# A decoder layer on one core: the w1/w3 products as seven block products for eight, w2 in a stage of its own, and the last normalisation moved into attention

## What is computed

```python
x = x + attn(layernorm(x), Wqkv, q_ln, k_ln, Wout)     # 32 heads of 32, ALiBi, causal
x = x + xattn(layernorm(x), ctx, Wq, Wk, Wv, Wo, bo, g) # softmax on q and k, normalised output
x = x + ffn(layernorm(x), w1, s1, w2, s2, w3, s3)

def ffn(x, ...):                 # dim 1024, hidden 2752, 4-bit weights, a scale for each 64
    a = einsum('bsd,hd->bsh', x, W1)
    b = einsum('bsd,hd->bsh', x, W3)
    return einsum('bsh,dh->bsd', silu(a) * b, W2)
```

## Time and profile before

| what | value |
|---|---|
| median of 3 runs | 3301.26 us (3300.97 to 3302.31) |
| span of the profiled execution | 3302.6 us |
| granted TensorE clock, mean | 0.976 of full |
| attention, one turn in the middle | 72.7 us |
| feed-forward stage | 1812.3 to 3302.6 us |
| PE / DVE / ACT / POOL busy | 95% / 54% / 32% / 15% |

### The profile page before, as it was taken

The page is one execution under the profiler, slowest core; times in us unless marked ns, Lnnn a source line. Parts: engine busy times, 40 slices in busy tenths (PEclk is TensorE's granted clock), DMA queues, the critical chain, the costliest instruction groups (busy, mean ns, idle before and its releaser), DMA issues. The chain is left out here.

```text
span 3302.6 us, 41842 instructions
## 1 busy us (share of the span) xinstructions
PE 3132.5 (95%) x15136; PEld 2396.3 (73%) x15136; DVE 1772.9 (54%) x2927; ACT 1045.8 (32%) x2356; POOL 506.7 (15%) x525
## 2 busy tenths in 40 slices
PE   7999998799999999999996799999999899999999
PEld 6888886566666666666663688888887788888887
DVE  5311112466666666666663655555555655555555
ACT  2100000566666566666651211111111211111111
POOL 2100000233333333333332100000000100000000
PEclk9999999899999999999997899999999999999999
DMA  4222223111111111111110422222122521222222
GB/s 143 93 71 74 73 73 109 48 39 38 38 51 48 40 38 39 50 38 51 38 33 25 134 82 54 72 65 80 54 81 73 153 66 54 81 81 54 61 75 78
DMA packets 83350, 218.73 MB, mean 66 GB/s; under 512 B 11984, under 2 KB 18256, under 8 KB 81232
## 3 DMA queue, kind: packets, MB, share of 16 engines
q1 hardware_dynamic: 83280, 217.78, 21.7%
HBM read 175.79 MB, written 41.94 MB: 66 GB/s over the span
## 5 line engine op out<-in xcount | busy, mean ns | idle before, releaser
L1042 ACT ACTIVATE w_hi<-words 128x1024 fp32r<-128x1024 f32 x134 | 142.5, 1064 | 697.5 <-DVE words L1087 697.5
L312 PE MATMUL ff_ps<-h_xT_hi,w_hi 128*128 128x512 f32 x1376 | 344.0, 392 | 13.2 <-DVE h_xT_lo L96 13.2
L1127 DVE TENSOR_TENSOR acc<-ff_po,acc 128x512 f32<-128x512 f32 x352 | 243.0, 692 | 210.0 <-PE ff_po L1214 209.3
L312 PE MATMUL ff_ps<-h_xT_lo,w_hi 128*128 128x512 f32 x1376 | 341.8, 391 | 0.0
L312 PE MATMUL ff_ps<-h_xT_hi,w_lo 128*128 128x512 f32 x1376 | 339.8, 389 | 0.0
L312 PEld LDWEIGHTS ff_ps<-h_xT_hi,w_hi 128*128 128x128 f32 x1376 | 259.8, 189 | 68.4 <-issue 8.8
L312 PEld LDWEIGHTS ff_ps<-h_xT_lo,w_hi 128*128 128x128 f32 x1376 | 260.0, 189 | 54.4
L312 PEld LDWEIGHTS ff_ps<-h_xT_hi,w_lo 128*128 128x128 f32 x1376 | 258.3, 188 | 53.6
L282 DVE TENSOR_SCALAR qkv_out<-qkv_acc 128x512 f32<-128x512 f32 x96 | 66.4, 692 | 396.5 <-PE qkv_acc L312 396.5
L1115 DVE TENSOR_TENSOR gate<-gate,ff_ps 128x512 f32<-128x512 f32 (+1 forms) x88 | 60.3, 686 | 345.4 <-PE ff_ps L312 344.6
L656 ACT ACTIVATE scores<-scores,neg_max 128x128 f32<-128x128 f32 x512 | 199.1, 390 | 122.6 <-DVE neg_max L487 122.6
(11 more groups left out here) (156 smaller groups left out, 5196.5 us busy)
## 6 DMA issues: line engine op xcount, KB each, us to landing
words<-in_w SPq DMA_DIRECT2D x90, 512.0 KB, 3.5
qkv<-qkv_out SPq DMA_DIRECT2D x96, 256.0 KB, 2.0
words<-in_w SPq DMA_DIRECT2D x176, 128.0 KB, 4.0
sc<-in_s SPq DMA_DIRECT2D x88, 256.0 KB, 4.3
qk_in<-qkv SPq DMA_DIRECT2D x16, 1024.0 KB, 5.0
w_stage<-in_w_attn SPq DMA_DIRECT2D x56, 256.0 KB, 2.9
qkv_rows<-in_x SPq DMA_DIRECT2D x16, 512.0 KB, 3.8
ctx_in<-in_context SPq DMA_DIRECT2D x16, 512.0 KB, 3.8
```

The costliest lines, as they stand in the source:

```text
L312: last = nc.tensor.matmul(out, left, right, start=n == 0, stop=n == len(pairs) - 1)
L1042: nc.scalar.activation(dst, src, ACT.Copy).then_inc(s["split_hi"], 1)
L1127: nc.vector.tensor_tensor(cols, po[:, o % 4, :], cols, ALU.add).then_inc(s["added"], 1)
```

## The change

The feed-forward stage is written anew. For a whole tile of units the four blocks w1 and w3 by lower and upper half of the columns are the left matrix, and two slices of 512 rows by lower and upper half of the columns are the right one. Seven block products with sums of blocks on both sides give what eight gave. Left blocks (A11, S1, S2, A12, S3, S4, A22) go as high and low parts into a ring of 10 slots; four of them are sums that POOL makes (left_sums). The right operands of a half are the blocks b11, b21 and b22 (R11, R21, R22 of `raw`, loaded from DRAM) and the differences t1 to t4, made by DVE and POOL once per half; all seven are split into high and low parts of 2048 columns. Three results of a tile add up in one PSUM bank, `chain`: ACT copies the bank out (`snap`) after A11, after S2 and after S3, and PE goes on adding to it. DVE combines the copies with the banks b, c and d. The last tile of a half stays direct (merged_tile, 24 + 36 matmuls). The gated units are stored to DRAM (`hid`) and read back by a w2 stage after all tiles, in 6 chunks of four tiles (the last of two), each by 4 groups of 512 rows; all of x2 is loaded as `acc` there. All of it is written out, without loops. In attention, each x2 is also normalised and transposed and stored to DRAM as `xt`, two turns later, at steps 2 (DVE), 3 (POOL) and 4 (PE, ACT) of the turn; the last one after the turns. Turn 1 is written out, and the loop starts at 2.

```diff
+    def post_statistics(dve, b):
+        dve.wait_ge(s["fin"], b - 1)
+        nc.vector.bn_stats(x2_st[:, 0:6], res[:, 0:N])
+        nc.vector.bn_stats(x2_st[:, 6:12], res[:, N:D]).then_inc(s["x2_stats"], 1)
...
+    def post_normalise(pool, b, projected):
+        pool.wait_ge(s["x2_mom"], b - 1)
+        nc.gpsimd.tensor_tensor(x2_mo[:, 4:5], x2_mo[:, 3:4], neg8[:, 0:1], ALU.pow).then_inc(s["x2_rstd"], 1)
+        pool.wait_ge(s["x_done"], projected)
+        pool.wait_ge(s["x2_rstd"], b - 1)
+        hold_pool()
+        nc.gpsimd.tensor_scalar(x2n[:, :], res[:, :], x2_mo[:, 2:3], x2_mo[:, 4:5], ALU.add, ALU.mult).then_inc(
+            s["x2_norm"], 1)
+
+    def post_turn(pe, b):
+        pe.wait_ge(s["x2_norm"], b - 1)
+        for k in range(KT):
+            last = nc.tensor.transpose(pair_k[:, k * P:(k + 1) * P], ln_columns(x2n[:, :], k), ident[:, :])
+        last.then_inc(s["x2_turned"], 1)
+
+    def post_copy(act, b):
+        act.wait_ge(s["x2_turned"], b - 1)
+        nc.scalar.activation(flat(x2t[:, :, :]), pair_k[:, :], ACT.Copy).then_inc(s["x2_copied"], 1)
+
+    def post_store(sp, b):
+        sp.wait_ge(s["x2_copied"], b - 1)
+        sp.dma_start(xt[b - 2, :, :, :], x2t[:, :, :]).then_inc(s["xt_stored"], 16)
...
+    def turn_tensor(pe, b, own, cross, ahead, post):
+        c = b - 1
         for t in range(STEPS):
+            if post and t == 4:
+                if own:
+                    pe.wait_ge(s["kt_out"], b * XT + 2)
+                post_turn(pe, b)
...
         @block.sync
         def _(sp):
+            def load13(u):
+                if u >= 2:
+                    sp.wait_ge(s["w_lo"], base(u - 1))
...
+            sp.wait_ge(s["ab_done"], base(TILES - 1))
+            load2(0)
+            load2(1)
+            load_hidden(0)
+            load2(2)
+            load2(3)
+            store(TILES - 1)
+            load_hidden(1)
+            sp.wait_ge(s["ab_done"], base(TILES))
+            for t in range(NB):
+                sp.dma_start(acc[:, t, :], x2[t, :, :]).then_inc(acc_in[t // SETS], 16)
+            for m in range(CHUNKS2 * SETS):
+                if 4 + m < NT:
+                    load2(4 + m)
+                if 2 <= m + 2 < CHUNKS2 * SETS:
+                    load_hidden(m + 2)
...
+            def load_right(hf):
+                if hf:
+                    sp.wait_ge(s["ab_done"], base(NT - 1))
+                for at in (R11, R12, R22, R21):
...
         @block.gpsimd
         def _(pool):
+            def left_sums(v):
+                w = [words[v % 2][:, i, :].bitcast(F32) for i in range(2)]
...
+                nc.gpsimd.tensor_tensor(sums[:, 0, :], w[1][:, 0:N], w[1][:, N:D], ALU.add).then_inc(s["summed"], 1)
...
+            def right_sums(hf):
+                pool.wait_ge(s["x_t1"], hf + 1)
+                pool.wait_ge(r_in[R22 - R21], (hf + 1) * 64)
+                nc.gpsimd.tensor_tensor(raw[:, 1, :], raw[:, R22, :], raw[:, 0, :], ALU.subtract).then_inc(s["x_t"], 1)
+                pool.wait_ge(s["x_t"], 3 * hf + 1)
+                pool.wait_ge(r_in[0], (hf + 1) * 64)
+                pool.wait_ge(s["x_lo"], OPS * hf + 1)
...
         @block.scalar
         def _(act):
+            def snap(u, n):
+                act.wait_ge(s["ab_done"], base(u) + 2 * n + 1)
+                if n == 0 and u >= 2:
+                    act.wait_ge(h_stored[u % 2], stored_before(u - 1, u % 2))
+                nc.scalar.activation(ends[u % 2][:, n, :], chain[u % 2], ACT.Copy).then_inc(s["snapped"], 1)
...
+            hidden_high(0)
+            w2_high(0)
+            silu_merged(TILES - 1, 0)
+            w2_high(1)
+            w2_high(2)
+            silu_merged(TILES - 1, 1)
+            w2_high(3)
...
+            for m in range(CHUNKS2 * SETS):
+                if m + 1 < CHUNKS2 * SETS:
+                    hidden_high(m + 1)
+                if 4 + m < NT:
+                    w2_high(4 + m)
...
         @block.vector
         def _(dve):
+            def start_half(hf):
+                first = hf * NT
+                first_difference(hf)
+                left_low(first, A11)
+                right_low(hf, 0, b11, R11)
+                right_low(hf, 1, t1, 0)
...
+            unpack2(0)
+            unpack2(1)
+            gate_merged(TILES - 1, 0)
+            w2_low(0)
+            w2_low(1)
+            unpack2(2)
+            hidden_low(0)
+            gate_merged(TILES - 1, 1)
+            unpack2(3)
+            w2_low(2)
+            w2_low(3)
+            for m in range(CHUNKS2 * SETS):
+                add(m, 0)
+                if 4 + m < NT:
+                    unpack2(4 + m)
+                add(m, 1)
+                add(m, 2)
+                if m + 1 < CHUNKS2 * SETS:
+                    hidden_low(m + 1)
...
         @block.tensor
         def _(pe):
+            def terms(u, j, op):
+                at = slot(u, j)
+                (hi, lo) = op
+                return [(l[:, at, k * P:(k + 1) * P], r[:, :, k, :])
+                        for l, r in ((ring_hi, hi), (ring_hi, lo), (ring_lo, hi)) for k in range(HK)]
...
+            def whole(u):
...
+                into = (a, bank_c, a, bank_b, a, bank_d, a)
+                ready = (1, 2, 3, 4, 6, 5, 7)
+                for j in range(OPS):
+                    pe.wait_ge(s["w_lo"], base(u) + j + 1)
+                    if first:
+                        pe.wait_ge(s["x_lo"], OPS * hf + ready[j])
...
+                    if j in (S2, S3, A22):
+                        pe.wait_ge(s["snapped"], 3 * k + {S2: 1, S3: 2, A22: 3}[j])
+                    multiply(into[j], terms(u, j, right[j]), j in (S2, S3, A22))
+
+            def merged_tile(u):
+                pe.wait_ge(s["w_lo"], base(u) + 2)
+                pe.wait_ge(s["h0_done"], u - 1)
+                multiply(chain[u % 2], terms(u, 0, b11) + terms(u, 1, b21))
+                pe.wait_ge(s["combined"], 4 * whole_before(u) - 2)
+                multiply(bank_b, terms(u, 0, t1) + terms(u, 0, b11) + terms(u, 1, b22))
...
+            def outputs(m):
+                q = m // SETS
+                n = inner(q)
+                pe.wait_ge(s["h_ready"], m + 1)
+                pe.wait_ge(s["w2_done"], 4 * q + n)
```

More of the change, by code:

```diff
@@ L1239, in lay_out_ffn @@
+            for u in range(TILES):
+                if merged(u):
+                    merged_tile(u)
+                else:
+                    whole(u)
+            for m in range(CHUNKS2 * SETS):
+                outputs(m)
+    keep.close()
 def lay_out_ffn(w1, s1, w2, s2, w3, s3):
```

735 lines of the change are left out of this document (467 added, 268 removed).

## The result

The changed kernel takes 3295.85 us (median of 14 runs, 3294.48 to 3297.84); the kernel before, in the same rounds, 3302.73 us. The ratio is 0.998, 95% interval [0.9972, 0.9987]: faster by 0.2%, where I had predicted 3242 us and no less than 3203, no more than 3290. The profiled span is 3292.9 us, so against my sum of 3243.7 some 49 us are missing.

What follows compares the result with a forecast made beforehand. TensorE was taken to bound the kernel, almost alone in feed-forward and near its limit in attention. -108.8 + 39 - 3.5 - 9.3 + 30 - 6.3 = -58.9 gave a 3243.7 us span, 3242 on the median; range 3203 to 3290.

Steps and rivals of the forecast that it cites:

- Matmuls removed: Feed-forward stage: 480 fewer matmuls at 0.2267 us, 108.8 us gone if PE never waits inside a tile.
- rival 2: PE waits inside each whole tile: 3284 us at 1 us a tile, slower past 1.4; chance 0.14, a third of it slower.
- the sum of 17.3 under 19.04: Whole tile: DVE's 12.1 us and POOL's 5.2 fully in series would still fit the tile's 19.04 us.
- Attention: Attention turns: moved-in normalisation and transposes cost 2.4 us for 14 turns, 5 in the last, +39; bounds 14 and 80.
- Start: Feed-forward start: first product at 16 to 18 us, first tile ended at 46; loss 27, with the 7 34 for 37.5.
- The bound of 48: Feed-forward start: high bound of the loss, with DVE and POOL wholly in series.
- rival 4: The w2 opening and both half starts at their high bounds (50, 48, 30): 3289 us; chance 0.08.
- the 24 us of DVE: Start of a half: seven 2048-wide low parts, the difference and seven of 512, in series on DVE behind the data.
- Between halves: From first to second half: PE idles some 7 us, restarts at half clock, waits for t3; 17 us for 26.3, bounds 12 and 30.
- w2 opening: Start of the w2 stage: PE idle 19.4 us plus 3 for half clock, then 5 to 8; +30, bounds 20 and 50.
- End: Kernel's end: one addition and one store, 5 us for 11.3, -6.3; bounds 4 and 9.
- rival 1: Slower through PE's new wait in attention, deciding from 6.5 us a turn; 7.5 us would give 3318; chance 0.08.

Runs made afterwards that it cites:

- the two runs with step 9: Changed kernel, attention's x2 transposes moved from step 4 to 9: in all turns 3291.23 us; only in turns with a next block 3291.09 us.

## Why the prediction was wrong

- **Matmuls removed, -108.8: right.** Whole tiles of 19.05 us without a gap; rival 2 (waits inside a tile) does not occur once a half is under way. The exclusion of DVE and POOL costs nothing there, but by a thinner margin than the sum of 17.3 under 19.04 said: POOL's five instructions take 1.26 to 1.29 us each and not 1.04, which makes 12.1 + 6.3 = 18.4 us, an estimate from these rows.
- **Attention, +39 and 7 to the stage's start: right in size, 47.3 for 46, in part by luck.** The last copy oT_hi of ACT came 41.1 us later than before (1767.5 for 1726.4), where I had 34 for the turns, and what lies behind it grew by 6.2, where I had 5 + 7. The two misses cancel. The wait for kT was there as predicted (1.0 for 1.1), but the two runs with step 9 show that removing it saves only 0.5 us a turn, so as the cause of a turn's loss it is not borne out.
- **Start, loss 27: this step failed, 45.8 (18.8 more).** I had put the end of the first tile at 46 us after the stage's start; it ended at 64.8 (1924.3). The bound of 48 was for this loss and the 7 together, as rival 4's 14 over 34 shows, so for an end at 60, with DVE and POOL wholly in series; measured are 45.8 + 7 = 52.8. The trace gives the path. DVE's first difference begins at 12.8 us (I had the data at 10.5). The low word of b22 is done 31.3 us later: 16.2 us of DVE's own instructions up to there and POOL's three differences of 4.94 us, 31.0 in series, an estimate that adds up the times which they take when not held. Then 4.4 us go to ACT's copies for t3 and t4 and the bank's copy behind them, and from S2 to the end of the tile PE takes 16.3. So, first, I had written the exclusion down and then let the two engines work in parallel in the forecast; moving the differences to DVE gave 14.0 us over both halves, although DVE then had 6.8 us more to do in each. Second, copies of the chain's bank stand on ACT behind work that waits for others; I had followed this link in the steady tile only. The runs show that it decided which product waited, not when the tile was done, and that is the third term: the 24 us of DVE were right for the first tile (22.7 in the trace), but once the bank's copy is out of the way, S3 and A22 stand behind the second tile's unpacking (4.1) and through it behind low words and combines (up to 4.8 by then), which leaves next to no room ahead of A22.
- **Between halves, loss 17: failed for the same reason, 34.0 (17 more; the bound was 30).** There the third difference took 13.95 us, and A22 began 48.3 us after DVE's first difference. The 7.1 us of idle PE after the merged tile were right.
- **w2 opening, loss 30: under-sized, 44.0 (14 more), within its bound of 50.** Each wait was named, as were its queue mates. The first hole was 27 us for 19.4. The path had the hidden chunk landing 11.7 us after the last whole tile; it landed at 16.9, since SP issued twelve other loads first, and the third w2 tile landed at 30.1, not 22. The second hole was 11.6 for 5 to 8, as the x2 loads began at 2789.6 and not 29 us after the last whole tile (2781.7), because SP stood behind the store of the merged tile's last unit, which DVE gated at 2788.7. The pace of these loads was as predicted, 412 GB/s from 2795 to 2812. Each restart of PE ran at the lower clock.
- **End, 5: right** (3.8, just under its low bound of 4).
- **The range.** Rival 4 had all three openings at their high bounds and gave 3289 with a chance of 0.08. The result lies 7 us past it. Only 2 of these are in the span (its 128 for the openings with the 7, measured 130.8); 4 come from taking the median to lie 1.3 us below the span, where it lies 3.0 above (the profiled execution itself took 3294.65 us). The start and the stretch between the halves share a cause, so they did not miss independently as a chance of 0.08 assumes. In rival 1, 3256 + 15 x 5 is 3331 and not 3318; 3318 is 3242 + 15 x 5.1. Nothing else rests on it.

## What to carry to other kernels

A change that trades matmuls for elementwise work pays at every place where the pipeline is empty, not in the steady part: there, add up every instruction of the busiest elementwise engine until the first tile is done, the next tile's included. If it exceeds TensorE's time, expect little from reordering: four orders here gave the same A22 within 0.3 us, and 3.5 us more work moved it by 5.5. That less work would gain as much is likely, but no run here shows it. If two engines exclude each other, add their times at such a place instead of taking the longer. When an experiment makes one product earlier and the end does not move, ask how busy the engine behind it is before moving the next wait. And check that the start of a gauge does not move itself.

## What the runs showed of the hardware that I had not expected

- A POOL difference of 2048 columns took 4.94 us when DVE stood still for it, and 13.95 when DVE ran one instruction behind the other for its first 9.6 us. Two such differences stretched a pair of DVE instructions from 1.28 to 10.06 us. One with 512 columns took 1.26 to 1.29 us, where one with a broadcast operand took 1.04.
- A one-operand product with a constant took POOL 5.36 us for 2048 columns with DVE idle, while a normalisation of 1024 columns with two operations took 1.20. Why stays open.
- Each hole costs more than its length. Behind holes of 4 to 11 us, eight matmuls took 3.2 to 3.8 us instead of 1.98; taking away a hole of 11.6 us gave 15.2 of span, 14.7 by the gauge.
- Attention's end, its code unchanged, differed by 3.9 us between kernels that differ only in later code, 2.8 of it in the last turn, by how long TensorE stayed on its lower clock. What sets this was not found; a comparison of two kernels by spans alone would have put it down to the edit.
